# Attention outputs of a Perceiver layer through memory instead of through TensorE's transposes, with a moved tail table

## The reference, cut to what matters

```
def xattn(query, key, value):                # keys and values from the context
    Q, K, V = (t.reshape(B, T, 16, 16).transpose(0, 2, 1, 3) for t in (query @ Wq.T + bq, ...))
    out = einsum('bhst,bhtd->bhsd', softmax(Q K / 4), V)
    out = out.reshape(B, T_src, D_MODEL)     # no transpose back: rows are (head, 16 positions)
    return out @ Wh.T + bh
def attn(x):                                 # causal linear attention over 64 features
    ctx = einsum('bhtf,bhtfd->bhtd', q_ch, cumsum(k_f * v)); den = maximum(..., 1e-06)
    return (ctx / den) reshaped to (B, T, C) @ Wout + bout
x = x + xattn(layernorm(x), ctx, ctx)
x = x + attn(layernorm(x))
x = x + ffn(layernorm(x))                    # silu(x wg) * (x wu), then wd; 768 hidden, int8-range weights
```

## Time and profile before

| | |
|---|---|
| median of 3 runs (lowest, highest) | 877.13 us (877.02, 878.48) |
| profiled execution: time, span of the trace | 875.48 us, 873.8 us |
| PE busy | 829.1 us, 95% |
| ACT busy | 541.5 us, 62% |
| DVE busy | 417.2 us, 48% |
| busiest DMA queue (SP's), share of the 16 engines | 38.3% |
| chain that ended last | PE 82%, DVE 8%, issue 4%, DMA 2%, ACT 2% |

### The profile page before, as it was taken

The page is one execution under the profiler, slowest core; times in us unless marked ns, Lnnn a source line. Parts: engine busy times, 40 slices in busy tenths (PEclk is TensorE's granted clock), DMA queues, the critical chain, the costliest instruction groups (busy, mean ns, idle before and its releaser), DMA issues.

```text
span 873.8 us, 20543 instructions
## 1 busy us (share of the span) xinstructions
PE 829.1 (95%) x8817; PEld 569.8 (65%) x8817; DVE 417.2 (48%) x746; ACT 541.5 (62%) x598; POOL 47.1 (5%) x76
## 2 busy tenths in 40 slices
PE   6899999999999998999999998999999999989876
PEld 5666666666666666676666665667666666657656
DVE  7433236444644445534654446354474444402654
ACT  2478887776577665667567764575657666672141
POOL 1034000000000000000000000000000000000010
PEclk9899999999999999999999999999999999999999
DMA  7486654646344333346343441443614333202000
GB/s 248 172 258 237 241 183 166 209 158 193 122 146 146 142 125 133 122 133 191 136 146 145 146 142 53 158 158 129 195 65 170 122 122 119 100 2 50 0 2 15
DMA packets 58768, 120.08 MB, mean 137 GB/s; under 512 B 21552, under 2 KB 29744, under 8 KB 55152
## 3 DMA queue, kind: packets, MB, share of 16 engines
q1 hardware_dynamic: 56880, 114.31, 38.3%
q0 software_dynamic: 1792, 4.40, 1.7%
HBM read 78.84 MB, written 37.75 MB: 133 GB/s over the span
## 4 chain that ended last, share of the span: by engine, by line
PE 82%; DVE 8%; issue 4%; DMA 2%; ACT 2%; DVEq 1%; POOL 1%; SPq 0%; POOLq 0%; ACTq 0%
PE ps_o L816 26%; PE ps_s L828 18%; PE ps_pa L662 10%; PE ps_pa L617 10%; PE ps_pa L763 2%; PE ps_pa L692 2%; PE ps_pa L788 2%; PE ps_pa L775 2%; PE ps_pa L754 1%; ACT probs L1258 1%; PE ps_pa L740 1%; DMA oscr<-y 1%; PE ps_pa L684 1%; PE ps_pa L795 1%; PE ps_pa L767 1%
## 5 line engine op out<-in xcount | busy, mean ns | idle before, releaser
L1258 ACT ACTIVATE probs<-ps_s 128x1024 f32<-128x1024 f32 x512 | 496.8, 1023 | 234.2 <-PE ps_s L828 227.7
L816 PE MATMUL ps_o<-probs,values 128*17 128x256 f32 x4096 | 256.1, 385 | 0.0
L828 PEld LDWEIGHTS ps_s<-qstack,kstack 64*128 64x128 f32 x2048 | 140.0, 186 | 99.6 <-ACT probs L1258 48.8
L828 PE MATMUL ps_s<-qstack,kstack 64*128 64x256 f32 x2048 | 194.0, 307 | 5.3 <-ACT probs L1258 5.3
L816 PEld LDWEIGHTS ps_o<-probs,values 128*17 128x17 f32 x4096 | 104.1, 98 | 98.7 <-issue 9.8
L1343 DVE TENSOR_SCALAR kparts<-ps_pa,b_heads 128x512 fp32r<-128x512 f32 x64 | 48.0, 750 | 107.4 <-PE ps_pa L617 107.1
L662 PE MATMUL ps_pa<-wv_hi,ctx_hi 128*128 128x256 f32 x256 | 79.6, 311 | 2.9 <-DVE wv_lo L1331 2.2
L1360 DVE TENSOR_TENSOR values<-ps_pa,bv_pair 128x512 f32<-128x512 f32 x64 | 44.2, 690 | 77.5 <-PE ps_pa L662 77.1
L662 PE MATMUL ps_pa<-wv_lo,ctx_hi 128*128 128x256 f32 x256 | 72.5, 283 | 0.0
L662 PE MATMUL ps_pa<-wv_hi,ctx_lo 128*128 128x256 f32 x256 | 72.4, 283 | 0.0
L617 PE MATMUL ps_pa<-ctx_hi,wk_hi 128*128 128x512 f32 x128 | 56.4, 441 | 0.0
(11 more groups left out here) (274 smaller groups left out, 786.7 us busy)
## 6 DMA issues: line engine op xcount, KB each, us to landing
kstack<-kscr SPq DMA_DIRECT2D x96, 512.0 KB, 5.3
kscr<-kparts SPq DMA_DIRECT2D x64, 512.0 KB, 2.7
ctx_raw<-ctxT SPq DMA_DIRECT2D x32, 512.0 KB, 6.5
qstack<-qscr SPq DMA_DIRECT2D x12, 256.0 KB, 3.5
qscr<-qparts SPq DMA_DIRECT2D x4, 512.0 KB, 3.1
xh<-x SPq DMA_DIRECT2D x4, 256.0 KB, 5.4
kstack<-kstack SPq DMA_DIRECT2D x2, 512.0 KB, 6.0
qstack<-ksample SPq DMA_DIRECT2D x4, 256.0 KB, 3.6
```

What stands on the lines that cost most here:

```text
L816: last = mm(ps_o[32 * j:32 * j + DH + 1, g * S:(g + 1) * S], values[par][:, i, head_of_step(g, j), :], prob[:, j * S:(j + 1) * S], start=b ...
L828: last = mm(ps_s[s % 2][:, j * S:(j + 1) * S], kstack[par][rows, u, i * P:(i + 1) * P], queries[rows, u, :], start=True, stop=True)
L1258: nc.scalar.activation(probs[n % AHEAD][:, :], ps_s[n % 2][:, :], ACT.Exp, scale=float(DH) ** -0.5).then_inc(fast["exp_done"], 1)
```

## The change

**The first attention** no longer goes through PE. `o_sb` is written as it stands, head by head in four DMAs of 32 partitions (pieces of 1 KB), by `write_heads`; it is read back with positions on the partitions (`read_rows`, two DMAs in pieces of 64 bytes, 17 rows each with the denominators). The new DVE stage `on` (step 9) waits for it, takes the reciprocals, does the range check of the denominators and scales into `y`. `oT0` and `oT1` are gone; `yT` stays at 12, `wh` at 13.

**The second attention** goes by `turn_values`: at pass 5 SP waits for `pv3`, writes `o_sb` in four DMAs, waits for them, and reads the denominators (sent to every partition) and the rows, already transposed. The new DVE stage `o2n` (step 92) scales them into `xT`. `o2T0`, `o2T1` and `y2T` are gone; the rows of `wout` are loaded in the order that fits.

**Layernorms** are stages of their own (`ln1`, `ln2`) behind `wh` and `wout` on DVE; the signal of `wh` and `wout` is now given before the layernorm, not behind it. **Steps:** `wout` 92 to 94, `ln2T` 96 to 99, `gu0` 99 to 100, head `ln0T` 94 to 92, `q` 100 to 98. ACT takes `gu0` and `gu2` one exponential earlier in their quad, `gu5` too.

**The last tail:** four writes from SP and ACT, two reads with one semaphore each, no `oT`; its second attention stays on PE. `last_down` becomes two passes of the rounded type over the parts of `hid`, and DVE makes the parts (`cut`, two more operations per `gate`). `warm` counts are 34 ahead of `yT` (12 and 26 before) and 6 behind `wh`.

```diff
-AT = {"o": 1, "oT0": 3, "oT1": 4, "yT": 12, "wh": 13, "ln1T": 19, "qk0": 20, ...
+AT = {"o": 1, "on": 9, "yT": 12, "wh": 13, "ln1": 13, "ln1T": 19, "qk0": 20, ...
-      ... "pv3": 84, "o2T0": 86, "o2T1": 88, "y2T": 90, "wout": 92,
-      "ln2T": 96, "gu0": 99, "gate0": 101, "gu1": 102, "gate1": 103, ...
+      ... "pv3": 84, "o2n": 92, "wout": 94, "ln2": 94,
+      "ln2T": 99, "gu0": 100, "gate0": 101, "gu1": 102, "gate1": 103, ...
...
-ACT_BEHIND = {n: 1 - AT[n] % 2 if AT[n] // QUAD in WIDE_QUADS else QUAD - 1 - AT[n] % QUAD for n in FEATS + GATES}
+ACT_BEHIND = {n: 1 - AT[n] % 2 if AT[n] // QUAD in WIDE_QUADS else QUAD - 1 - AT[n] % QUAD for n in FEATS}
+ACT_BEHIND.update({n: (QUAD - 2 if AT[n] % QUAD < 2 else QUAD - 1) - AT[n] % QUAD for n in GATES})
...
+        def write_heads(eng, c, j):
+            t, e = j // CI, j % CI
+            eng.dma_start(oscr[t].rearrange("d (g e) s -> e d g s", e=CI)[e],
+                          o_sb[32 * j:32 * j + 2 * DH, :, :]).then_inc(c["o_written"], 16)
...
             def write_output(c, clock):
-                wait_all((c["operand"], c.at("operand", clock, "oT1")))
+                wait_all((c["operand"], c.at("operand", clock, "o")))
+                for j in range(GH):
+                    write_heads(sp, c, j)
+            def read_rows(t, landed):
+                sp.dma_start(o_rows[:, t, :, :], oscr[t, 0:DH + 1].rearrange("d h (a u) -> (h a) d u", u=DH)).then_inc(landed, 16)
             def regroup_output(c, tails):
+                wait_all((c["o_written"], tails * (16 * GH) + 16 * GH))
                 for t in range(ST):
-                    sp.dma_start(oscr[:, t * P:(t + 1) * P, :].rearrange("h s d -> s h d"),
-                                 y[:, t, :].rearrange("p (h d) -> p h d", h=H)).then_inc(c["o_written"], 16)
...
+                    read_rows(t, c["o_in"])
+            def turn_values(c, clock, tails):
+                wait_all((c["operand"], c.at("operand", clock, "pv3")))
+                for j in range(GH):
+                    sp.dma_start(o2scr.rearrange("d (g j) s -> j d g s", j=GH)[j],
+                                 o_sb[32 * j:32 * j + 2 * DH, :, :]).then_inc(c["o2_written"], 16)
+                wait_all((c["o2_written"], tails * (16 * GH) + 16 * GH))
+                sp.dma_start(o2_den, o2scr[DH:DH + 1].to_broadcast([P // H, H, S])).then_inc(c["o2_in"], 16)
+                sp.dma_start(o2_rows, o2scr[0:DH].rearrange("(i e) h s -> (e h) i s", i=CI)).then_inc(c["o2_in"], 16)
...
+                elif name == "on":
+                    dve.wait_ge(c["o_in"], clock[1] * (16 * ST) + 16 * ST)
+                    if c is fast and tails:
+                        dve.wait_ge(c["stored"], tails * 16)
+                    v.reciprocal(rden[:, :, :], o_rows[:, :, DH, :])
+                    check_rows()
+                    for t in range(ST):
+                        last = scaled_rows(t)
+                elif name == "o2n":
+                    dve.wait_ge(c["o2_in"], clock[1] * 32 + 32)
+                    v.tensor_scalar(o2_den, o2_den, 1e-6, None, ALU.max)
+                    dve.drain()
+                    v.reciprocal(o2_den, o2_den)
+                    dve.drain()
+                    last = v.tensor_tensor(xT[:, :, :], o2_rows, o2_den.unsqueeze(1).to_broadcast([P, CI, S]), ALU.mult)
                 elif name in ("wh", "wout"):
-                    v.tensor_tensor(xs[:, :, :], xs[:, :, :], bank[:, :].rearrange("p (t d) -> p t d", t=ST), ALU.add)
-                    dve.drain()
+                    last = v.tensor_tensor(xs[:, :, :], xs[:, :, :], bank[:, :].rearrange("p (t d) -> p t d", t=ST), ALU.add)
+                elif name in ("ln1", "ln2"):
                     last = layernorm(c, name, clock)
...
                 for t in range(ST):
-                    last = mm((ps_p, ps_a)[t][:, 0:D], hid[:, k, t * P:(t + 1) * P], wd_sb[:, k, :],
-                              start=k == 0, stop=k == HB - 1)
+                    for part in range(2):
+                        last = mm((ps_p, ps_a)[t][:, 0:D], last_part(k, part)[:, t * P:(t + 1) * P], wd_r[:, k, :],
+                                  start=k + part == 0, stop=k + part == HB)
...
-                v.scalar_tensor_tensor(hid[:, k, :], gate_e[:, k % 2, :], 1.0, hid[:, k, :], ALU.add, ALU.mult
-                                       ).then_inc(last_vector, 1)
+                v.scalar_tensor_tensor(hid[:, k, :], gate_e[:, k % 2, :], 1.0, hid[:, k, :], ALU.add, ALU.mult)
+                dve.drain()
+                if k >= HALF // 2:
+                    dve.wait_ge(*product_of(f"gu{HB - 1}"))
+                cut(last_part(k, 0), last_part(k, 1), hid[:, k, :]).then_inc(last_vector, 1)
```

More of the change, by code:

```diff
@@ L102 @@
 WIDE_QUADS = {AT[n] // QUAD for n in WIDE}
-ACT_BEHIND = {n: 1 - AT[n] % 2 if AT[n] // QUAD in WIDE_QUADS else QUAD - 1 - AT[n] % QUAD for n in FEATS + GATES}
-NEEDS = {"maxT": "max3", "oT0": "o", "oT1": "o", "qk1": "ln1T", "v": "ln1T", "qkT0": "norm0", "qkT1": "norm1",
+ACT_BEHIND = {n: 1 - AT[n] % 2 if AT[n] // QUAD in WIDE_QUADS else QUAD - 1 - AT[n] % QUAD for n in FEATS}
+ACT_BEHIND.update({n: (QUAD - 2 if AT[n] % QUAD < 2 else QUAD - 1) - AT[n] % QUAD for n in GATES})
+NEEDS = {"maxT": "max3", "qk1": "ln1T", "v": "ln1T", "qkT0": "norm0", "qkT1": "norm1",
          **{n: "qkT1" for n in FEATS}, **{f"A{p}": "qkT1" for p in range(H // 2)},
-         **{f"pv{g}": f"A{2 * g + 1}" for g in range(G)}, "o2T0": "pv3", "o2T1": "pv3",
+         **{f"pv{g}": f"A{2 * g + 1}" for g in range(G)},
          **{f"gu{k}": f"gate{k - 2}" if k >= 2 else "ln2T" for k in range(HB)},
@@ L723, in stage @@
                                   ident[:, :], start=True, stop=True, skip_group_check=True)
-                elif kind in ("oT", "o2T"):
-                    for g in range(G):
-                        last = nc.tensor.transpose(bank[:, g * P:(g + 1) * P], o_sb[:, g, n * P:(n + 1) * P],
-                                                   ident[:, :])
                 elif name == "yT":
-                    pe.wait_ge(c["o_in"], clock[1] * 16 + 16)
-                    last = transpose_blocks(bank, y)
-                elif name == "y2T":
                     last = transpose_blocks(bank, y)
@@ L786, in down_part @@
                 for t in range(ST):
-                    last = mm(bank[:, t * D:(t + 1) * D], hid[:, k, t * P:(t + 1) * P], wd_sb[:, k, :],
+                    last = mm(bank[:, t * D:(t + 1) * D], hid[:, k, t * P:(t + 1) * P], wd_r[:, k, :].bitcast(FP32),
                               start=k + t == 0, stop=k == HB - 1, skip_group_check=True)
@@ L1190, in stage @@
                     weighted(c, FEATS.index(name), clock)
-                elif name in ("ln0", "wh", "wout"):
+                elif name in ("ln0", "ln1", "ln2"):
                     power(c, name, clock)
@@ L1286, in _ @@
                                  ).then_inc(last_scalar, 1)
+            act.wait_ge(*vector_of("o0"))
+            act.wait_ge(*scalar_of("o1"))
+            for j in range(CI, GH):
+                write_heads(act, fast, j)
             last_columns("yT1", "yT1", halves[3])
@@ L1449, in stage @@
                     last = v.tensor_copy(xhT[:, :, :], bank[:, :].rearrange("p (i s) -> p i s", i=CI))
-                elif name in ("ln1T", "yT", "y2T"):
+                elif name in ("ln1T", "yT"):
                     last = v.tensor_copy(xT[:, :, :], bank[:, :].rearrange("p (i s) -> p i s", i=CI))
```

186 lines of the change are left out of this document (78 added, 108 removed), and 4 rows, old and new, of the table AT.

## The result

The changed kernel takes **886.22 us** (median of 9 runs, 882.6 to 888.44), the kernel before 877.8 us in runs beside it (9 runs, 874.97 to 882.3). The ratio is 1.0083, 95% interval 1.0057 to 1.011: slower by 0.8%, where the prediction had 874.5 and a range of 866 to 884. The profiled execution took 883.44, with a span of 881.7 against 873.8 before: 7.9 us more to be found.

The account below looks back on a forecast made before the run. It took a ring of PE's scores and ACT's exponentials, not PE alone, to set each quad. Terms summed to -6.75 us, with +4.1 for the clock -2.65, so 877.13 became 874.5 us, range 866 to 884.

Parts of the forecast that it names:

- The wait at yT: Quad of `yT`: PE waits 3.2 us for `y` (bounds 1.0 and 5); +8.4 us over three batches.
- The clock: Behind five new PE waits (three of 3.2 us, two of 2.1): falls at two, 2 us each, +4.1 us.
- rival 1: At `yT`: waits of 4.3 us and three clock falls of 3.3, about 883; chance 0.31 together with rival 4.
- rival 4: Second attention: the reciprocal or `o2_in` late by 1.5 us, three times, 879; chance 0.31 together with rival 1.
- Start of a batch, pass 5: Quads losing `oT0`, `oT1`: -2.7 us; quads with `pv3` and `o2T`: -4.2 us; each over three batches.
- Behind wout: Quad of `wout` and the one behind: PE's layernorm wait goes, `ln2T` waits 2.1 us; -3.5 us in all.
- almost no wait: At `wout`: `o2n` is ready at 332.7 and PE comes at 333.2, so PE hardly waits.
- the whole trip lies behind work: Second attention: reads land at 329.4 to 329.9, DVE is in its keys until about 329.65, hiding the trip.
- The quads behind in the last batch: Fourth batch, behind the `wout` quads: no head or `q` to trade, only slack and `gu2`; -1.0 us.
- the three terms of passes 5 and 6: `pv3` and `o2T` quads -4.2 us; `wout` and the quad behind -3.5; the quads after those -4.4 and -1.0.
- Last tail: End of the kernel: `y` turned earlier, -1.7 us ahead; DVE's `cut` delays the output, +2.35; together +0.65 us.
- Rival 2: First trip short enough: `y` at 210.3 to 211, waits 1 to 1.5 us, no fall; about 866, chance 0.17.

Follow-up runs that it names:

- The run with the dummies: The changed kernel with 15 dummy products on PE ahead of each wait for `y` at `yT`: 880.88 us, ratio to before 1.0036.

## Why the prediction was wrong, point by point

**The wait at yT** is the step that failed, in its size and in what it drags along. The mechanism, the place, the number (three) and the engine that releases it were as written. The term was +8.4 with a wait of 3.2 us. Measured are 3.9, 4.5 and 4.2, so the three waits came to 12.5 us, not 9.6. In the second batch `y` stood at 213.8, not 212.6: 0.5 us is the writes (landed at 206.4, not 205.9) and 0.8 the reads (5.2 us, not 4.4); `on` took 2.25 us (2.3 predicted). PE itself came 0.65 us later than written, so the wait grew by 0.7. I had taken "a little less" than the write in pieces of the earlier trace rows; it was a little more. And two of my reasons for the lengths fall with the runs: moving `x` behind the writes did not shorten them (7.6 us for 7.4), and the pieces of 64 bytes are 0.8 us of the read. Four writes of the same shape took 4.4 us at pass 5, so some 3 us of the 7.4 belong to the place; the loads of keys, which I had named as being ahead, are the likely reason, but no run tests it.

**The clock.** I had written that each of the three waits is longer than the one that cooled the array in the earlier trace rows, and then counted a fall at two of five. There was one behind each of the three, at 1.6, 2.4 and 2.1 us, and none behind the two of 1.1 us at `ln2T`, nor behind the wait of 1.0 at wout in the last batch. Applied as it stood, that reading gives three falls at 2 us, about +6; I had discounted it without a row. In all the traces here, each of PE's 13 waits of 2.7 us and more between the second batch's start and the last tail is followed by a fall; of the eight from 2.0 to 2.4 us five are and three are not, with the same wait on both sides, so there the count is luck. A fall in the last tail (1.1 us) I did not foresee. The price of one was about right (2 us). Together the three quads of yT are longer by 17.6 us, where the sum had 8.4 and at most the 4.1 of the clock. That is rival 1 (883), which together with rival 4 I had at 0.31: it had a wait of 4.3 us and three falls of 3.3. Its threshold was written too high: with three falls at 3.3 us the sum passes 878.9 at the wait of 3.2 us already (874.5 + 5.8), so by its own prices the slow side deserved more than I gave it. The run with the dummies shows the falls apart from the wait.

**Start of a batch, pass 5.** Right: -3.3 for -2.7, -4.1 for -4.2.

**Behind wout.** Right in the second batch: 16.00 us, 15.9 predicted; in the third -2.8 for -3.4. The reciprocal of 256 columns took 1.75 us for 1.7. `ln2T` waited 1.1, not 2.1, as it came later: PE waited 0.5 to 1.0 for what stands behind `o2n` on DVE, which I had as "almost no wait". In the last batch, where no head hides it, wout waited 1.0 us for `xT`. And the sentence that the whole trip lies behind work did not hold: DVE stood idle 3.0 us in three for the read, and its own part of the trip gives back 2.4 us. The quads behind in the last batch gave +0.5 for my -1.0, which has nothing to do with the trip: with the moves alone it is +0.6, because `gu0` went from slot 99 into the next quad; the quad that it left is 1.3 us shorter.

**The attribution** was not a step with a number, but the sum hid it: the three terms of passes 5 and 6 are not the worth of the second trip. 8 of 10 us come with the moved slots alone.

**Last tail.** The front was 1.3 us less good than written: `y` 0.9 later (the trip as above) and `wh` at the lower clock. DVE's cut cost 2.1, 2.35 predicted.

**The rivals.** Rival 2 (a short trip) is excluded by the 5.2 us of the read, which even whole rows bring only to 4.4; its sum is 864.9, not 866. The 2.6 us that the prediction works out for the reads from the Trainium skill, "DMA: Bandwidth & Descriptors", section "Anatomy of one DMA", are excluded as well; the page gives that fit for DMAs issued by GpSimd, and these are SyncE's. Rival 4 came in part: the reciprocal took what was written, the read came late by 0.6 to 1.3 us of DVE's time.

**The noise.** The 0.2% between "faster" and "no change" was read from three runs. Nine runs of the same kernel lie between 874.97 and 882.3 us, 0.8%, so single runs could not have told a change of -2.65 us from none.

## What to carry to other kernels

Where products leave PE for a trip through memory, move what needs the result by the length of the trip, and then look at the stage behind it: a single slot (`qkT1`) was worth 8 us. Price an idle stretch of PE at itself and the fall of the clock behind it; if the profile of before shows a fall behind a shorter wait, count one behind every longer one (here that held 13 times of 13 from 2.7 us up), and take shorter waits as open. And time the moved slots without the new mechanism before crediting the mechanism: here they were 8 of the 10 us of one half. Three kernels beat both that were compared by 7 to 8 us: the moves alone (870.5 us), with the second trip (868.9), and with both trips and the stages spread (869.2), so that the first trip, even repaired, adds nothing that can be measured.
